# One place later for the next batch's row transposes, and with them its modulation and split

## What is computed

```python
mod = (_silu(c) @ wmod).reshape(32, 6, 1, -1)          # sa, ca, ga, sb, cb, gb
h = _layernorm(x) * (1 + ca) + sa
q, k, v = givens_rotate(rot_w[0], h), givens_rotate(rot_w[1], h), givens_rotate(rot_w[2], h)
attn = softmax((2.0 + 2.0 * cin) / scale + bias)        # cin: q against k, a row of zeros in front
ave = einsum('bhqk,bhkd->bhqd', attn, v)
x = x + ga * ave / sqrt(clip(abs(sum(ave * ave)), 1e-08))
h = _layernorm(x) * (1 + cb) + sb
# 16 experts with 512 hidden features, each takes the best 64 rows of every batch; and a shared one
x = x + gb * (scattered expert outputs + (gelu(h @ Wsg) * (h @ Wsu)) @ Wsd)
```

## Time and profile before

| what | value |
|---|---|
| runs | 2466.6 us median of 3 (2465.52 to 2469.54) |
| span of the profiled execution | 2465.3 us |
| what lies around the span, against the median | 1.3 us |
| TensorE matmuls | 2372.3 us busy, 96% of the span |
| TensorE weight loads | 2086.3 us, 85% |
| VectorE, ScalarE, GpSimd | 64%, 42%, 47% busy |

### The profile page before, as it was taken

One profiled execution on the slowest core, in us unless ns is written; L12 is line 12 of the kernel. 1 busy time (PEld: TensorE's weight loads), 2 busy tenths in 40 slices (PEclk: granted clock), 3 DMA queues, 4 the chain that ended last, 5 costly groups with the idle time before them and its releaser, 6 DMA issues.

```text
span 2465.3 us, 40995 instructions
## 1 busy us (share of the span) xinstructions
PE 2372.3 (96%) x14388; PEld 2086.3 (85%) x14388; DVE 1567.9 (64%) x3198; ACT 1032.8 (42%) x1912; POOL 1150.4 (47%) x997
## 2 busy tenths in 40 slices
PE   6999999999998999999987999999999999999997
PEld 5888888888887888888876888888888888888886
DVE  6677767778776877788846455555554545555553
ACT  3545545444553545545442333333333333333332
POOL 1233333333332333333352666666666666666664
PEclk9999999999998999999998999999999999999999
DMA  2111111111111111111115444443444444434433
GB/s 90 53 44 59 51 60 60 52 51 57 54 61 44 60 43 60 52 60 60 59 62 90 86 90 82 88 84 66 79 84 87 86 85 88 84 60 86 84 62 43
DMA packets 78506, 167.03 MB, mean 68 GB/s; under 512 B 11744, under 2 KB 46720, under 8 KB 78368
## 3 DMA queue, kind: packets, MB, share of 16 engines
q0 software_dynamic: 49152, 67.14, 16.7%
q1 hardware_dynamic: 29216, 97.85, 11.8%
HBM read 97.71 MB, written 67.24 MB: 67 GB/s over the span
## 4 chain that ended last, share of the span: by engine, by line
PE 84%; DVE 6%; issue 4%; POOL 2%; DMA 1%; ACT 1%; SPq 0%; DVEq 0%; POOLq 0%; ACTq 0%
PE ps L349 26%; PE ps L351 26%; PE ps L350 26%; PE ps L501 2%; DVE stage L856 2%; PE ps L387 1%; DVE bn_stats L758 1%; PE ps L420 1%; DMA stage<-in_wd 1%; DVE x_t L753 1%; PE ps L442 1%; DVE hidden L753 1%; POOL rstd L1144 1%; POOL out L1209 1%; ACT x_t L693 0%
## 5 line engine op out<-in xcount | busy, mean ns | idle before, releaser
L349 PE MATMUL ps<-x_t,weights 128*128 128x512 f32 x1536 | 617.3, 402 | 23.2 <-DVE hidden_f L1111 13.3
L350 PE MATMUL ps<-x_t,weights 128*128 128x512 f32 x1536 | 602.5, 392 | 0.0
L351 PE MATMUL ps<-x_t,weights 128*128 128x512 f32 x1536 | 601.8, 392 | 0.0
L1209 POOL DMA_INDIRECT out<-x_rows,step_token x256 | 418.1, 1633 | 333.9 <-DVE x_rows L1090 275.4
L349 PE MATMUL ps<-weights,hidden 128*128 128x256 f32 x1536 | 435.8, 284 | 8.7 <-POOL hidden L1148 5.6
L351 PE MATMUL ps<-weights,hidden 128*128 128x256 f32 x1536 | 436.1, 284 | 0.0
L350 PE MATMUL ps<-weights,hidden 128*128 128x256 f32 x1536 | 436.0, 284 | 0.0
L1111 DVE TENSOR_TENSOR hidden_f<-gelu,ps 128x512 f32<-128x512 f32 x256 | 175.7, 686 | 379.0 <-ACT gelu L733 348.1
L733 ACT ACTIVATE gelu<-ps 128x512 f32<-128x512 f32 x256 | 152.8, 597 | 535.8 <-PE ps L351 508.4
L349 PEld LDWEIGHTS ps<-x_t,weights 128*128 128x128 f32 x1536 | 290.6, 189 | 83.6 <-DVE hidden_f L1111 13.5
L1148 POOL TENSOR_TENSOR hidden<-hidden_f,hidden 128x512 fp32r<-128x512 f32 x128 | 165.5, 1293 | 408.7 <-ACT hidden L647 408.7
(11 more groups left out here) (174 smaller groups left out, 4436.9 us busy)
## 6 DMA issues: line engine op xcount, KB each, us to landing
x_rows<-in_x SPq DMA_DIRECT2D x32, 512.0 KB, 3.5
pairs<-mod_rows SPq DMA_DIRECT2D x32, 512.0 KB, 4.3
h_rows<-stage SPq DMA_DIRECT2D x32, 512.0 KB, 2.6
out<-y_rows SPq DMA_DIRECT2D x32, 512.0 KB, 2.9
stage<-in_wg SPq DMA_DIRECT2D x16, 512.0 KB, 3.4
stage<-in_wd SPq DMA_DIRECT2D x16, 512.0 KB, 4.4
stage<-in_wu SPq DMA_DIRECT2D x16, 512.0 KB
x_rows<-h_rows,step_token POOLq DMA_INDIRECT x256
```

Of the source, the lines that this page charges most:

```text
L349: pe.matmul(o, lhs(HI), rhs(HI), start=start, stop=False)
L350: pe.matmul(o, lhs(HI), rhs(LO), start=False, stop=False)
L351: return pe.matmul(o, lhs(LO), rhs(HI), start=False, stop=stop)
L1209: pool.indirect_dma_start(out=out_rows, out_offset=bass.IndirectOffsetOnAxis(ap=ICUR[g][:, t:t + 1], axis=0), in_=X1[:, g % 2, t * D:(t + ...
```

## The change

In three engines' `iteration` the work on the next batch goes one place later, and one wait is written out ahead of `top_best(1)`.

```diff
@@ TensorE
                 if valid(i):
                     a_times_v(i, 0)
+                if valid(i - 1):
+                    gate_up(i - 1, 1)
+                if valid(i):
+                    a_times_v(i, 1)
                 if valid(i + 1):
                     x_transposes(i + 1)
                 if at(i, -1):
                     modulations()
-                if valid(i - 1):
-                    gate_up(i - 1, 1)
-                if valid(i):
-                    a_times_v(i, 1)
                 if finish is not None:
                     top_transposes(finish)
@@ ScalarE
                 if valid(i):
                     squares(i, (0, 1))
+                if valid(i - 1):
+                    hidden(i - 1, 1)
+                if valid(i):
+                    squares(i, (2, 3))
                 if valid(i + 1):
                     h1_modulate(i + 1)
-                if valid(i - 1):
-                    hidden(i - 1, 1)
-                if valid(i):
-                    squares(i, (2, 3))
                 if valid(i - 1):
                     hidden(i - 1, 2)
@@ VectorE
                 if start is not None:
                     group_scores(start)
+                if valid(i - 1):
+                    hidden(i - 1, 1)
+                if len(rounds) > 1:
+                    dve.wait_ge(top_kept, rounds[1][2])
+                    top_best(1)
+                if valid(i):
+                    out_norm(i)
                 if valid(i + 1):
                     h1_split(i + 1)
-                if valid(i - 1):
-                    hidden(i - 1, 1)
-                if len(rounds) > 1:
-                    top_best(1)
-                if valid(i):
-                    out_norm(i)
                 for g, r, before in rounds[1:]:
                     top_strike(1, g, r, before)
```

More of the change, by code:

```diff
@@ L704, in iteration @@
                     squares(i, (0, 1))
-                if valid(i + 1):
-                    h1_modulate(i + 1)
                 if valid(i - 1):
@@ L710, in iteration @@
                     squares(i, (2, 3))
+                if valid(i + 1):
+                    h1_modulate(i + 1)
                 if valid(i - 1):
@@ L1060, in iteration @@
                     group_scores(start)
-                if valid(i + 1):
-                    h1_split(i + 1)
                 if valid(i - 1):
@@ L1068, in iteration @@
                     out_norm(i)
+                if valid(i + 1):
+                    h1_split(i + 1)
                 for g, r, before in rounds[1:]:
```

## The result

The changed kernel takes 2527.7 us, the median of 4 runs (2520.4 to 2532.7), against 2468.1 (2465.5 to 2471.4, 4 runs) for the kernel before on the same chip: a ratio of 1.0238 with a 95% interval of 1.0223 to 1.0252, so slower by some 59.7 us. The prediction was 2520 with a range of 2503 to 2540.

What follows compares the result with a forecast made beforehand. TensorE, with 84% of the chain that ended last, was taken to bound the kernel. The profiled span of 2465.3 us, plus 53.4 of added waits and 1.3 around the span, gave 2520.0 us, range 2503 to 2540.

Steps and rivals of the forecast that it cites:

- The wait taken away: TensorE's row transposes (L387) no longer wait for VectorE's normalisation (L856): worth up to 0.62 us an iteration.
- The wait that takes its place: gate_up group 1 waits for VectorE's multiply of hidden group 0; TensorE on balance 0.49 us worse off an iteration.
- The chain uncovered: Transposes, modulation, rounding and split take 4.71 us against 3.65 of cover; the next K product waits 1.06 us each iteration.
- The upper bound of the chain: Transposes to K product at most 5.04 us, with ScalarE late by some 0.14 and the split by 0.19.
- One iteration: From group 0's multiply's end to the next K product: 10.65 us instead of 9.10, so +1.55 us an iteration.
- The rule against the change: VectorE and GpSimd share ports: the rounding might wait 0.19 us for GpSimd's power, making the sum 59.1 instead of 53.4.
- The sum: Extra time added over all iterations, including 3.0 us for iteration 0 and 6.6 for 10, 18 and 26: 53.4 us.
- Granted clock unchanged: Sign expected in the changed profile: TensorE's granted clock stays as before; a fall inside the loop would refute the forecast.
- The rival on the clock: TensorE's gaps halve its clock for one gate group in half of the iterations: 43 us more, 2563; chance 0.05.
- the chain is covered: Modulation and split take under 3.65 us, so only the wait for the multiply is left: 2482 us; chance 0.03.
- the delay is absorbed: The K product slips by 1.55 us once and the period of 38.2 us stays: 2468 us; chance 0.04.
- it gets faster: Group 1 starts at 500.44 and the chain is hidden, so 0.62 us an iteration is gained: 2448 us; chance 0.02.

Runs made afterwards that it cites:

- experiment 1: Against the kernel before: transposes, modulation and split moved behind gate_up group 1 only, still ahead of the second half of A times V; 2480.8 us, ratio 1.0047.
- experiment 8: Against the changed kernel: GpSimd's add of the output rows moved ahead of its two small operations for the normalisation; 2494.4 us, ratio 1.0109 to the kernel before.
- experiment 7: Against the kernel before: GpSimd's add of the output rows moved ahead of its two small operations for the normalisation; 2444.8 us, ratio 0.9905.
- Experiment 9: Against the kernel before: transposes, modulation and split moved behind gate_up group 1 only, and GpSimd's add moved ahead; 2447.0 us, ratio 0.9927.
- experiment 3: Against the changed kernel: modulation, rounding and split handed over in halves between ScalarE and VectorE; 2515.3 us, ratio 1.0188 to the kernel before.
- experiment 2: Against the changed kernel: VectorE's multiply of hidden group 0 moved ahead of the normalisation; 2508.4 us, ratio 1.0147 to the kernel before.
- experiment 4: Against the changed kernel: TensorE back in its old order, ScalarE and VectorE left in the new one; 2582.4 us, ratio 1.0470 to the kernel before.
- experiment 5: Against the kernel before: transposes, modulation and split behind gate_up group 1 only, and group 0's multiply ahead of the normalisation; 2464.4 us, ratio 0.9984.

## Why the prediction was right

Both parts of the mechanism hold, and the experiments separate them. From the pairs that differ in one of them alone:

| part | from | us |
|---|---|---|
| wait for the multiply in place of the wait for the normalisation | experiment 1 against before | 11 |
| chain uncovered, with the waits for the score rows and the clock's falls | experiment 8 against experiment 7 | 49.6 |
| both | changed kernel against before | 59.7 |

They add up to 60.6, so little is left for a third cause. Experiment 9 leaves nothing for a place behind group 1 as such; the last place, behind the second half, was run only with the chain bare.

*The wait taken away.* Right: the row of L387 is gone.

*The wait that takes its place.* Right in kind: group 1 starts 0.15 us behind the multiply's end, 0.14 was assumed. In size it was a little less: 0.35 to 0.4 us an iteration in the middle of the loop in experiment 1 where 0.49 was priced, 11 us in all where 30 x 0.49 is 15. Part of the difference is the small wait of group 2 for group 1's multiply (experiment 7), which the new order takes away and the prediction left out.

*The chain uncovered.* Right: 4.79 us where 4.71 were taken from iteration 0. The 0.08 us more are ScalarE's: the squares' last accumulator read is at 537.42, and the modulation starts 537.59 - (536.38 + 1.04) = 0.17 us behind the transposes' end instead of 0.10. The transposes as cover were 0.79 us (536.38 to 537.17) where 0.81 were taken. In size it was a little more: 1.26 us an iteration between experiments 7 and 8 where 1.06 was priced. The longer chain and the shorter cover are 0.11 of this; the other 0.1 is on TensorE, where V starts 1.46 us behind a K product that had waited and 1.36 behind one that had not. (The upper bound of the chain had 0.14 us for the accumulator read; the rows that it names give 0.10.)

*One iteration.* From the multiply's end to the next K product 541.17 - 530.51 = 10.66 us; the prediction had 10.65. That it agrees so closely is luck: the chain was 0.08 us longer than assumed, and the second half 0.08 shorter (536.38 - 533.50 = 2.88 where 2.96 were taken, which held the wait of group 2). The other part of the loop, which was left at 29.15, is 530.51 - 501.27 = 29.24. So the period grew by 1.65 us where 1.55 was forecast: the first part a little cheaper, the second a little dearer, and over 30 iterations some 3 us too few.

*The rule against the change.* It did not apply: the power ended 0.16 us before the rounding began, which is where the prediction had placed it ("just clear"). The rounding took 0.69 us as before. Nor would it have cost what was put on it. Where the two do meet, the rounding is hardly held up: in experiment 3 its first half took 0.43 us beside the power, and the power waited. In experiment 2 they meet in 20 iterations, and the rounding took 0.69 to 0.72 us. So the 0.19 us, and the sum of 59.1 built on it, price a wait that these runs do not show; besides, the prediction's own terms, with 2.61 us from transposes to rounding as in the earlier trace rows, put the rounding at 501.55 + 2.84 + 2.96 + 2.61 = 509.96 and not at 509.87, which leaves 0.10.

*The sum.* Here is the step that was mis-sized. "Granted clock unchanged" holds in every ordinary iteration, but not behind the long K waits. Iteration 0 and the three that end on the score rows were priced by their waits alone, 3.0 and 6.6 us, and those waits came out at 2.8 and 6.6. What the waits bring with them was left out: the half clock behind them, some 9.5 us. The evidence for the steady clock was a gap of 1.04 us, good for the ordinary iteration's gap of 1.0 us and not for gaps of 2.1 to 3.7. The gap of 3 us that the prediction itself put into iteration 0 was never set beside a gap of that length, though the trace before has a longer one, 5.2 us ahead of iteration 19, with 17 us of half clock from 743.4 on. The rival on the clock looked for it in the wrong place, in half of all iterations. Experiment 4 shows that it was close to true: with gaps of 1.8 us a third of the iterations lose the clock.

*The rivals.* That the chain is covered, that the delay is absorbed, that it gets faster: each has its counter-row above (a wait of 37.3 us, a period of 39.9, a multiply that ends where it did).

Of the experiments' expectations four were missed by 10 us or more in ways that count: number 2 by the search rounds on VectorE and by the clock, number 5 by the rounds, number 3 by VectorE's own share of the chain, number 4 by the clock. Number 7 and number 8 did better than expected, by 10 and 11 us. That one swap on GpSimd takes the wait for the normalisation, or for the multiply behind it, out of all three orders is shown; and experiment 9 shows no gain of the smaller move on top of it.

## What to carry to other kernels

A step that is moved later on one engine costs nothing until the work left behind it is shorter than the chain that hangs on it: add up that chain over all its engines from a place where it stands bare, and compare it with the cover that the new order leaves. When a wait is taken away, look what else ran late for the same reason and had been hidden by that wait; here it was the multiply right behind the normalisation, which held up group 1 as soon as the transposes no longer stood ahead of it. And a normalisation that is late is better mended where it is late (one instruction on GpSimd, 24 us) than by an order in which its reader comes later.

## What the runs showed of the hardware that was not expected

- Gaps on TensorE and its clock. Behind gaps of about 1.0 us (two in each ordinary iteration of the changed kernel) the granted clock never fell inside the loop. Behind gaps of 1.8 to 1.9 us in experiment 4 it fell from 1.00 to 0.50 in 9 of 27 iterations. Ten K products in all the traces waited 2.1 to 3.2 us for the score rows. Behind six the clock fell: 2.11 and 2.39 us in the changed kernel, 2.14 and 3.19 in experiment 2, 3.20 in experiment 4, 2.11 in experiment 8. Behind four it did not: 2.21 in experiment 3, 2.91 in experiment 4, 2.97 in experiment 5, 2.39 in experiment 8. So a gap's length alone doesn't decide it in these runs, and what else does was not tried. A fall costs 1.4 to 4.9 us here.
- One VectorE instruction an iteration that stood beside one of GpSimd's took up to 2491 ns instead of some 400. Taking it away gave 24 us in the kernel before, and 33 in the changed kernel (2527.7 to 2494.4), which waits for more that comes behind it.
- Which of the two waits is not settled by which began first. GpSimd's add had begun 0.06 us ahead of that piece, and the piece waited. GpSimd's power had begun 0.64 us ahead of the rounding in experiment 3, and the power waited: 1.10 us instead of 1.02. In experiment 2, 4 of the 20 powers that met the whole rounding took 1.57 us and ended 0.04 us behind it; the other 16 took 1.02, and the rounding then 0.71 to 0.72 instead of 0.69. What makes the difference was not tried.
- The norm's product (L877) took 0.34 to 0.42 us in 20 iterations of the kernel before, beside GpSimd's product of L1148, and 0.16 us in all of the changed kernel, where that product runs earlier.
